# Second half of a two-layer kernel: the first unit's stack rows moved by head pair, the first batch's rectified parts made on VectorE, and the key logarithm taken sooner

## The reference, cut to what matters

```
q_mag, k_mag = softplus(q), softplus(k)
q_embed = [q_mag * cos(freqs), q_mag * sin(freqs)]
k_embed = [k_mag * cos(freqs + bias), k_mag * sin(freqs + bias)]
scores  = q_embed . k_embed / sqrt(8);  out = softmax(scores) @ v @ wo
```

## Time and profile before

| | |
|---|---|
| runs | 1351.19, 1361.86, 1364.24 us; median 1361.86 us |
| profiled execution | 1352.82 us, of which the span of the profile is 1351.0 us |
| granted TensorE clock of the profiled execution, mean | 0.848 of full speed |
| second half | from about 467 us (memset of KS) to the end |

### The profile page before, as it was taken

The page is one execution under the profiler, slowest core; times in us unless marked ns, Lnnn a source line. Parts: engine busy times, 40 slices in busy tenths (PEclk is TensorE's granted clock), DMA queues, the critical chain, the costliest instruction groups (busy, mean ns, idle before and its releaser), DMA issues.

```text
span 1351.0 us, 16146 instructions
## 1 busy us (share of the span) xinstructions
PE 974.8 (72%) x5318; PEld 524.8 (39%) x5318; DVE 877.3 (65%) x1343; ACT 698.3 (52%) x1039; POOL 592.2 (44%) x585
## 2 busy tenths in 40 slices
PE   6464477877778525487687777787999987777884
PEld 5221234444434312132232223235888852323231
DVE  6572766665666555977878765645666668966861
ACT  3231245554554332567666467664344357667674
POOL 6367546677784263543612447650000035706210
PEclk9976688887888865579788798978999998889999
DMA  7713446645555118314312443535655634544400
GB/s 246 261 43 107 141 102 161 160 131 161 143 152 143 67 39 108 43 38 63 53 29 32 66 83 53 104 88 126 208 192 196 206 72 70 94 56 64 72 20 14
DMA packets 86482, 142.12 MB, mean 105 GB/s; under 512 B 14973, under 2 KB 43774, under 8 KB 86398
## 3 DMA queue, kind: packets, MB, share of 16 engines
q1 hardware_dynamic: 77726, 123.50, 38.1%
q0 software_dynamic: 8192, 16.79, 5.3%
q10 hardware_dynamic: 480, 0.79, 0.5%
HBM read 58.17 MB, written 40.37 MB: 73 GB/s over the span
## 4 chain that ended last, share of the span: by engine, by line
PE 31%; DVE 11%; ACT 10%; DMA 5%; SPq 4%; issue 4%; POOL 1%; ACTq 0%; DVEq 0%; POOLq 0%
PE PS L917 7%; PE PS L876 6%; ACT P L984 5%; PE PS L936 5%; PE PS L894 4%; SPq L497 4%; PE PS L856 3%; DMA KS<-MAG 3%; DVE MX L1729 3%; PE PS L842 2%; DVE XNT L1476 2%; PE PS L676 1%; PE PS L681 1%; ACT L984 1%; ACT MAG L984 1%
## 5 line engine op out<-in xcount | busy, mean ns | idle before, releaser
L1729 DVE TENSOR_REDUCE MX<-PS 128x2 f32<-128x1024 f32 x256 | 306.8, 1223 | 132.3 <-PE PS L856 126.4
L984 ACT ACTIVATE P<-PS 128x1024 f32<-128x1024 f32 x256 | 262.2, 1024 | 150.2 <-PE PS L894 144.9
L856 PE MATMUL PS<-KS,QS 62*128 62x512 f32 x512 | 142.3, 553 | 62.0 <-DVE MX L1729 49.6
L1312 POOL DMA_INDIRECT A<-Y1D,POS x64 | 61.8, 965 | 273.2 <-DMA Y1D<-YE 186.7
L894 PE MATMUL PS<-QS,KS 64*128 64x512 f32 x512 | 126.9, 491 | 73.7 <-ACT P L984 70.8
L876 PE MATMUL PS<-P,V 128*32 128x512 f32 x1024 | 157.9, 693 | 0.1
L856 PEld LDWEIGHTS PS<-KS,QS 62*128 62x128 f32 x512 | 55.0, 212 | 204.2 <-DVE MX L1729 106.2
L917 PE MATMUL PS<-XRH,WH 128*128 128x512 f32 (+1 forms) x276 | 103.8, 417 | 0.5 <-DVE A L1665 0.5
L894 PEld LDWEIGHTS PS<-QS,KS 64*128 64x128 f32 x512 | 54.6, 209 | 127.1 <-ACT P L984 116.5
L775 PE MATMUL PS<-XST,WB 128*128 128x512 f32 x184 | 99.6, 684 | 0.0
L1331 POOL DMA_INDIRECT XS1D<-XN,POS x64 | 61.6, 962 | 62.4 <-DVE MX L1729 41.3
(11 more groups left out here) (219 smaller groups left out, 1882.8 us busy)
## 6 DMA issues: line engine op xcount, KB each, us to landing
WH<-W1SD SPq DMA_DIRECT2D x23, 704.0 KB, 4.7
WS<-WD SPq DMA_DIRECT2D x64, 200.0 KB, 4.2
QS<-EH SPq DMA_DIRECT2D x64, 128.0 KB, 4.3
KS<-EH SPq DMA_DIRECT2D x60, 128.0 KB, 5.8
WB<-in_wb SPq DMA_DIRECT2D x23, 322.0 KB, 2.9
XS<-XS0D SPq DMA_DIRECT2D x23, 256.0 KB, 4.0
Y0D<-YE SPq DMA_DIRECT2D x23, 256.0 KB, 4.2
XS<-XS1D SPq DMA_DIRECT2D x23, 256.0 KB, 4.0
```

What stands on the lines that cost most here:

```text
L856: signal(pe.matmul(PS[:, s % 4, :], QS[rows, u % 3, hp, 128 * t:128 * t + 128], KS[rows, u % 3, hp, :], start=True, stop=True), "ms")
L984: act.activation(*a, **k).then_inc(sem[name], 1)
L1312: pool.indirect_dma_start(dst[:, k, t, :], None, src, bass.IndirectOffsetOnAxis(pos[:, k, g:g + 1], 0)).then_inc(sem[name], 16)
L1729: go("mx", dve.tensor_reduce(MX[:, u % 2, t].rearrange("p (o h) -> p o h", o=2)[:, :, hp], PS[:, s % 4 - 1:s % 4 + 1, :], AX.X, ALU.max))
```

## The change

The change touches only the start of the second half; every other batch and unit keeps its instructions.

1. Unit 0's 12 stack DMAs of 128 KB become 48 of 32 KB, one for each head pair j (`pair_rows`: 16 source partitions in steps of 4, 16 pieces of 2 KB). The 12 of head pair 0 count on a new semaphore stk_a, the other 36 on stk0. SP issues 6 and then 18, and ScalarE, in `first_keys`, 6 and then 18. `row_max(0, 0)` waits for stk_a, `row_max(0, 8)` for stk0. All later waits on stk0 count 24 more; `relu_abs(1, 2)` waits for stk_a as well.
2. For batch 0 the rectified part is made on VectorE (`tensor_scalar` max with 0.0 from the same bank, semaphore relu0), and ScalarE takes the absolute value after it.
3. The prologue's order becomes exp of keys, ln of keys, exp of queries, ln of queries, and for batch 0 the explicit table load at the key logarithm is left out.

```diff
-    out += [("exp", 0, 1), ("exp", 0, 0), ("ln", 0, 1), ("ln", 0, 0), ("mag", 0), ("hilo", 0), ("stack", 0), ("hout", 0),
+    out += [("exp", 0, 1), ("ln", 0, 1), ("exp", 0, 0), ("ln", 0, 0), ("mag", 0), ("hilo", 0), ("stack", 0), ("hout", 0),
...
+        def pair_rows(src, at, j):
+            return src[j:64:4, at, :]
...
-                                    load(dst[row:row + 16, u % 3].bitcast(F32), src[64 * half:64 * half + 64, at + par, :],
-                                         f"stk{u % 3}")
+                                    if u == 0:
+                                        load(dst[row:row + 16, 0, 0].bitcast(F32), pair_rows(src, at + par, 0), "stk_a")
+                                    else:
+                                        load(dst[row:row + 16, u % 3].bitcast(F32), src[64 * half:64 * half + 64, at + par, :],
+                                             f"stk{u % 3}")
+                if u == 0:
+                    for src, row, par in [(EH, 0, 0), (EH, 0, 1), (EH, 16, 0), (EH, 16, 1), (MAG, 32, 0), (MAG, 32, 1)]:
+                        for j in range(1, 4):
+                            load(QS[64 * par + row:64 * par + row + 16, 0, j].bitcast(F32), pair_rows(src, par, j), "stk0")
...
-                if i == 0:
-                    pe.wait_ge(sem[f"stk{u % 3}"], 16 * 12 * (u // 3 + 1))
+                if u == 0 and i == 0:
+                    pe.wait_ge(sem["stk_a"], 16 * 12)
+                if i == (0 if u else 8):
+                    pe.wait_ge(sem[f"stk{u % 3}"], 16 * (12 * (u // 3 + 1) + 24 * (u % 3 == 0)))
...
+                    if b == 1:
+                        act.wait_ge(sem["stk_a"], 16 * 12)
                     for u in (2 * b - 2, 2 * b - 1):
-                        act.wait_ge(sem[f"stk{u % 3}"], 16 * 12 * (u // 3 + 1))
+                        act.wait_ge(sem[f"stk{u % 3}"], 16 * (12 * (u // 3 + 1) + 24 * (u % 3 == 0)))
...
-                act.activation(EH[:, n, :], src, ACT.Relu)
+                if b:
+                    act.activation(EH[:, n, :], src, ACT.Relu)
+                else:
+                    act.wait_ge(sem["relu0"], (n + 2) % 4 + 1)
                 act.activation(MAG[:, n, :], src, ACT.Abs).then_inc(free, 1)
...
-                    if which:
+                    if which and b:
                         act.preload_act_table_set("natural_log_exp_and_others")
...
-                                act.dma_start(KS[row:row + 16, 0].bitcast(F32),
-                                              src[0:64, 2 + par, :]).then_inc(sem["stk0"], 16)
+                                act.dma_start(KS[row:row + 16, 0, 0].bitcast(F32),
+                                              pair_rows(src, 2 + par, 0)).then_inc(sem["stk_a"], 16)
+                                placed.append((src, row, 2 + par))
+                for src, row, at in placed:
+                    for j in range(1, 4):
+                        act.dma_start(KS[row:row + 16, 0, j].bitcast(F32), pair_rows(src, at, j)).then_inc(sem["stk0"], 16)
...
+                elif what == "qkev" and a[0] == 0:
+                    n = a[1]
+                    dve.wait_ge(sem["qk_first"], (n + 2) % 4 + 1)
+                    go("relu0", dve.tensor_scalar(EH[:, n, :], PS[:, n, :], 0.0, None, ALU.max))
+                    dve.wait_ge(sem["relu0"], (n + 2) % 4 + 1)
```

More of the change, by code:

```diff
@@ L262 @@
         "lsub hot eb pos gw gused lused gg lc a yev x1 h0 s_done gsum x0 step "
-        "rows01 stats1 xn1 lsub1 hot1 eb1 pos1 gw1 emb_q0 hi_q0 lo0 mx m2 fused ot gsum1 out emb_k0",
+        "rows01 stats1 xn1 lsub1 hot1 eb1 pos1 gw1 relu0 emb_q0 hi_q0 lo0 mx m2 fused ot gsum1 out emb_k0",
     "the last reader of a shared bank":
@@ L268 @@
         "wide0 wide1 staged split_out sent1 wh0 wh1 wd0 wd1 xs1_0 xs1_1 sto1_0 sto1_1 ygf "
-        "stk0 stk1 stk2 mst0 mst1 mst2 stored",
[1 row of a table added]
 }
@@ L1145, in first_keys @@
                 act.wait_ge(sem["rows01"], 2)
+                placed = []
                 for part, src in (("hi", EH), ("lo", MAG)):
```

## The result

The changed kernel takes 1363.79 us (median of 20 runs, 1352.2 to 1370.84) against 1356.88 us for the kernel before (20 runs on the same chip). The ratio is 1.0043, with a 95% interval of 1.0023 to 1.0063: 5.8 us more, 3.1 to 8.5. It is a small loss, and one that three runs could not have told from nothing.

What follows compares the result with a forecast made beforehand. The second half waited for unit 0's stack, with V's chain next. Softplus 2.1 us sooner and issues 11.5 us put the first reduce 6.0 us later, 5.5 taken: 1357.4 + 5.5 = 1362.9, say 1363; range 1352 to 1373.

Steps and rivals of the forecast that it cites:

- The second chain: Start of second half: V's eviction, logits and VectorE's steps end 3.4 us before the stack's chain and become late next.
- 18 issues at 0.64 us: ScalarE ahead of V: the added DMA issues hold the engine, 18 x 0.64 = 11.5 us.
- The softplus part: Batch 0 embedding: key logarithm 2.2 us sooner, rectified parts on VectorE cost 0.1 us; together 2.1 us sooner.
- The first reduce: VectorE's first row-max reduce: 528.0 against 522.03, 6.0 us later, 5.0 at the low end; 5.5 taken.
- the half microsecond that I had left open: ScalarE's key issues: V half a microsecond sooner if the one long issue of 1.14 us was an accident.
- The waits behind: After the first reduce: late head pairs covered by 5 us, unit 1's stack before `relu_abs(1, 2)` by 3.6 us.
- That the delay stays: From the first reduce on: each engine's list is the same, so 5.5 us stay to the end.
- The sign of being wrong: Profile of the changed kernel: the shift at the first reduce gone by 600 us, absorbed by later waits.
- Rival A: Issues on ScalarE and SP slow each other: first reduce 9.5 us late, at worst 15; 1366.9 to 1372.9; chance 0.15.
- Rival B: ScalarE not held or small issues much cheaper: V at 508.6, first reduce 5.5 us sooner; about 1356; chance 0.18.
- the next chain: Under Rival B, late head pairs and unit 1's stack: end between 3 us sooner and 1 us later.
- Rival C: Before ln of keys: a table load appears anyway, 1.28 us of gain goes; 6.8 us later, 1364.2; chance 0.10.

Runs made afterwards that it cites:

- e4: Kernel of e1 plus 18 issues of 8 bytes x 16 partitions on ScalarE behind the six key DMAs, ahead of V; ratio 1.0053.
- e7: As e4, with 54 in place of 18 tiny issues on ScalarE ahead of V; ratio 1.0257.
- e1: Kernel before with only the softplus reorder and the rectified parts on VectorE, stack still in 12 DMAs of 128 KB; ratio 0.999.
- a2_after_third: Changed kernel, no edit, measured a third time; ratio 1.0038.
- e3: Changed kernel with ScalarE's 18 DMAs of head pairs 1 to 3 moved behind the silu of batch 1; ratio 1.0014.
- e5: Changed kernel with ScalarE's key DMAs whole again, six of 128 KB, so only SP issues by head pair; ratio 1.0008.
- a1: Changed kernel, no edit, measured again beside the other runs; ratio 1.0006.
- e2: Changed kernel with the edits of e1 reversed: stack by head pair, softplus as before; ratio 1.0042.
- e6: Kernel of e1 with GpSimd's gathers of batch 2 moved behind the statistics of batch 1; ratio 0.9987.
- e6b: Same kernel as e6, measured once more; ratio 0.9984.

## Why the prediction was right

The forecast was 1363, 5.5 us above a base of 1357.4. Measured: 1363.79, 5.8 us more than before by the ratio, 3.1 to 8.5 by its interval. That the total came within 1 us is in part luck: the base, taken as the middle of four times and said to move by 6 us, was measured at 1356.88. What the runs test is the shift and its mechanism. Point by point:

- **The second chain.** That V's eviction and not the stack would be late next is what after shows: no wait for a DMA at the first row-max step, 24.2 us for V (23 forecast), and VectorE's four steps on the path.
- **18 issues at 0.64 us.** They ran from 508.43 to 519.94: 11.5 us, 0.64 each with its gap. e4 and e7 show that issues alone, with next to nothing in them, make the delay, and in proportion: 18 and 54 of them put the end of V 12.6 and 37.0 us behind that of e1.
- **The softplus part.** First embedding step 9.45 against 11.51: 2.1 us sooner, as forecast. The maximum on VectorE took 0.69 us where I took 0.65, and exp began at 7.22 against 7.09.
- **The first reduce.** 38.9 against 33.2, 5.6 us. The sum had 6.0 and the value taken was 5.5; the low key DMAs took 1.25 us in place of 1.72, which is the half microsecond that I had left open.
- **The waits behind.** `row_max(0, 8)` and `relu_abs(1, 2)` waited for no DMA; the latter came at 52.4, forecast 51.8. Unit 1's stack had landed by mark 45.2, where 537 (mark 48.2) was forecast: the cover was 7 us and not 3.6.
- **That the delay stays.** It was argued from the fixed lists alone, and that no slack gives any back was too strong: some 2 us of it are given back by mark 160 in both of its profiles, part of them at products that met the higher granted clock (under a2_after_third). The sign of being wrong, a shift gone by 600 us, did not come: it was 4.9 us there. The first pair of profiles seemed to speak against it: 7.8 us at the first reduce, 2.5 at the end. Between 600 and 700 us, core 0 of before and then of after (busy time of PE, PEld, DVE, ACT, POOL; granted clock; DMA share; GB/s):

```profile
600.00:700.00 100.00, 73.97 (x386) 29.54 (x386) 79.95 (x127) 71.39 (x92) 41.29 (x43) 0.83 0.32 47
```

```profile
600.00:700.00 100.00, 74.66 (x418) 30.22 (x414) 81.27 (x133) 73.59 (x95) 45.70 (x47) 0.89 0.33 49
```

  TensorE was granted 0.83 in before and 0.89 in after, and that is where after caught up: 3.4 us behind at mark 160, 0.5 us ahead at mark 178. a2 was granted 0.85 there and is still 3.0 behind at mark 178. With e7 it reads as the drift of single executions. What makes the grant differ there from one execution to another stays open.
- **Rival A, the two queues slow each other: out.** From 510.06 to 519.94 both queues issued without a break, ScalarE at 0.64 and SP at 7.61 / 12 = 0.63 us each. The Trainium skill, "Perfetto Trace Analysis", section "DMA Instruction — HWDGE (DVE, Sync)", has the descriptor generator locked for one DMA at a time. If that holds, the locked part is under some 0.32 us of each issue, since two queues together issued one every 0.32 us, and here it cost nothing. (The rival's sum gives 9.5 us and, at worst, 15.2; the time of 1366.9 fits the first, and the second would be 1372.6 and not 1372.9.)
- **Rival B, V not held:** made true by hand in e3 and e5. My point that the next chain catches it was right; how hard it catches was not. I had the first relu of batch 1 1 us behind before at most; it was 5.9 behind in the profile of e3 and 1.7 in that of e5. In e3 the step at fault is the landing of a DMA issued beside the stack of unit 1, taken from the shortest one seen, 3.4 us, where 7.9 us was measured. In e5 the stack of unit 1 was there at 48.1, the late end of the 535 to 537 (marks 46.2 to 48.2) that I had given; the slip was in the sum, for 537 is 1.9 us behind 535.12 and not 1.
- **Rival C, a table load after all:** none appeared.

## What to carry to other kernels

A DMA that a computing engine issues cost that engine some 0.6 us here, whether it moved 128 bytes or 128 KB: before a transfer is cut in four, read what stands behind the issues in that engine's list, and find the second-latest chain in front of the waiting instruction, because the gain ends there (here 3.4 us) and the cost starts there. A wait that is removed early in a pipeline is worth nothing if the same buffers are needed in full 20 us later; look for the bytes that compete with the late transfer instead (here eight gathers that could go later). Where a change is worth under half a per cent, marks counted from an untouched instruction close by are good to 0.5 to 1 us, while single spans, and even the ratio of 12 runs to itself, wander by 4 us.

## What the runs showed of the hardware that was not expected

- An issue took the same time whatever it carried: a median of 0.611 us for 16 pieces of 8 bytes (e4 and e7), 0.611 for 16 pieces of 2 KB (ScalarE's 18 in after), 0.624 for 64 pieces (ScalarE's four from EH in before). The means of 0.706 us in e4 and 37.48 / 54 = 0.694 in e7 come from single long issues: one of 1.81 us in e4, and in e7 four of 0.96 to 1.57.
- Such long issues, like the 1.14 us on ScalarE and the 1.81 on SP in before, need not come from two queues that issue side by side. SP's 1.81 began at 508.88, after ScalarE's last issue had ended at 508.81, and SP has others of up to 1.69 us later in before, when ScalarE issues nothing. Instructions on the tile QS, 600 to 1351 us of before (ns min/median/max):

```profile
L497 SPq DMA_DIRECT2D QS<-EH x52: 587/608/1692, 611.5 to 1264.2; - x52
```

  At the start of the second half they are gone where the stack of unit 0 goes by head pair on both queues (no issue over 0.72 us there in after, a1, a2, e2 and e3). They are shorter where the gathers come later (SP's fifth issue 1.21 and 1.31 us in e6 and e6b, 2.11 in e1). What makes an issue long stays open.
- The same eight products of the router logits took 1.88 us at a granted clock of 0.50 and 1.06 at 1.00, and both profiles of the changed kernel, some 5 us late at that place, have the second.
